# A four-layer transformer block in one kernel: first attention and first ffn with VectorE's side work moved and the up products computed a second time

## The reference, cut to what matters

```
# cond: x @ W_base + b_base + low rank part, weighted per batch
# attn: 16 heads of 8 features
q, k, v = proj(Wq) * mod, proj(Wk) * mod, proj(Wv) * mod
scores = einsum('bhid,bhjd->bhij', q, k) / sqrt(8) * cos_mat
w = softmax(scores); w = (w + roll(w, 1)) / sqrt(2)
x = x + einsum('bhij,bhjd->bhid', w, v) @ Wo

# cond2: a weight matrix per batch
w_bot = einsum('bg,got->bot', y, weight * mask)
y = einsum('bnt,bot->bno', x, w_bot) + bias

# ffn: everything is quantised with one scale per whole tensor
y = act_qdq(y)                      # scale = max(abs(y)) / 32767, round, scale back
up = act_qdq(y @ lpbq_dequant(w_up).T)      # 4 bit weights, a scale per 32 columns
gate = act_qdq(y @ lpbq_dequant(w_gate).T)
sig = fixed_qdq_u16(sigmoid(gate))
gate = act_qdq(gate * sig)
o = act_qdq(gate * up)
x = x + o @ lpbq_dequant(w_down).T
```

## Time and profile before

| what | value |
|---|---|
| median of 3 runs | 1338.44 us |
| lowest and highest run | 1337.14 and 1338.82 us |
| the profiled execution's own time | 1340.86 us |
| its span in the profile | 1339.0 us |
| PE, DVE, ACT, POOL busy in the span | 1201.0, 831.2, 652.2, 271.0 us |
| mean granted clock of PE | 0.98 of full |
| chain that ended last | PE 70%, DVE 18%, ACT 6% |
| first attention | about 24 to 157.4 us of the span |
| from its end to the first gate product | 157.4 to 166.3 us |
| first ffn | 166.3 to about 244 us |

### The profile page before, as it was taken

How to read it: one execution, slowest core, us unless ns; L and a number is a source line. 1 busy time by engine, 2 the same in 40 slices (tenths; PEclk the granted TensorE clock), 3 DMA queues, 4 the chain that set the end, 5 groups by cost and what they waited for, 6 DMA issues and landing times.

```text
span 1339.0 us, 28276 instructions
## 1 busy us (share of the span) xinstructions
PE 1201.0 (90%) x10379; PEld 965.6 (72%) x10379; DVE 831.2 (62%) x1749; ACT 652.2 (49%) x1334; POOL 271.0 (20%) x349
## 2 busy tenths in 40 slices
PE   5898762889999899999999999889999999989999
PEld 3666520458878789887887888479889866657777
DVE  4988678564555566657777565466564477764342
ACT  2766587345434234443454444234434467746553
POOL 4666200210004142330000014043330021200000
PEclk9999985999999999999999999999999999999999
DMA  9000100501312123104106101032102000000000
GB/s 328 2 2 2 49 31 0 212 0 64 133 81 89 52 64 98 48 25 161 53 17 257 48 8 50 22 94 78 44 20 88 1 2 3 3 3 0 1 16 16
DMA packets 42901, 75.86 MB, mean 57 GB/s; under 512 B 3849, under 2 KB 33809, under 8 KB 41873
## 3 DMA queue, kind: packets, MB, share of 16 engines
q1 hardware_dynamic: 38672, 65.66, 13.5%
q0 software_dynamic: 4096, 8.40, 2.1%
HBM read 59.75 MB, written 14.29 MB: 55 GB/s over the span
## 4 chain that ended last, share of the span: by engine, by line
PE 70%; DVE 18%; ACT 6%; issue 3%; DVEq 1%; DMA 1%; POOL 0%; ACTq 0%; SPq 0%; POOLq 0%
PE banks L1949 7%; PE banks L1960 7%; PE banks L1945 7%; PE banks L2004 5%; PE banks L1936 4%; PE banks L2014 3%; PE banks L1690 3%; PE banks L1685 3%; PE banks L1692 3%; PE banks L1691 3%; PE banks L1929 2%; PE banks L1931 2%; PE banks L1930 2%; DVE SM L2395 2%; PE banks L1816 2%
## 5 line engine op out<-in xcount | busy, mean ns | idle before, releaser
L2203 ACT ACTIVATE SC<-banks 128x512 f32<-128x512 f32 x192 | 114.4, 596 | 225.2 <-PE banks L1945 126.3
L2290 DVE SCALAR_TENSOR_TENSOR SC<-banks,SM,SC 128x512 f32<-128x512 f32 x128 | 95.9, 749 | 121.3 <-PE banks L1949 102.8
L1960 PE MATMUL banks<-A,SC 128*128 x1024 | 137.0, 277 | 8.3 <-DVE SC L2290 7.6
L1949 PE MATMUL banks<-X,SC 128*128 128x128 f32 x1024 | 136.9, 277 | 4.5 <-DVE SC L2569 3.2
L1945 PEld LDWEIGHTS banks<-X,SC 128*128 128x128 f32 x1024 | 126.1, 192 | 19.5 <-issue 12.5
L1945 PE MATMUL banks<-X,SC 128*128 128x128 f32 x1024 | 136.1, 276 | 4.4 <-ACT SC L2187 3.2
L1960 PEld LDWEIGHTS banks<-A,SC 128*128 128x128 f32 x1024 | 125.4, 192 | 17.8 <-issue 16.9
L1949 PEld LDWEIGHTS banks<-X,SC 128*128 128x128 f32 x1024 | 124.5, 192 | 6.9 <-DVE SC L2569 5.9
L2004 PE MATMUL banks<-A 128*128 128x128 f32 x736 | 100.0, 279 | 13.7 <-DVE A L2719 8.1
L2004 PEld LDWEIGHTS banks<-A 128*128 128x128 f32 x736 | 89.3, 191 | 19.1 <-ACT A L2228 9.7
L2187 ACT ACTIVATE SC<-A 128x512 f32 x128 | 80.6, 630 | 28.4 <-PE banks L1949 23.3
(11 more groups left out here) (342 smaller groups left out, 2518.0 us busy)
## 6 DMA issues: line engine op xcount, KB each, us to landing
A<-in_moe SPq DMA_DIRECT2D x36, 768.0 KB, 10.6
A<-xs SPq DMA_DIRECT2D x20, 256.0 KB, 3.9
ys<-A SPq DMA_DIRECT2D x20, 256.0 KB, 2.3
BW<-in_l1f SPq DMA_DIRECT2D x2, 2048.0 KB, 7.9
BW<-in_l2f SPq DMA_DIRECT2D x1, 3456.0 KB, 11.1
BW<-in_l1c SPq DMA_DIRECT2D x1, 3072.0 KB, 17.3
BW<-in_l3f SPq DMA_DIRECT2D x1, 2816.0 KB, 10.1
A<-in_l1c SPq DMA_DIRECT2D x1, 2560.0 KB, 8.7
```

Of the source, the lines that this page charges most:

```text
L1949: m = e.matmul(at["pu"].ap[:, cut(q)], wx[:, cut(4 + q)], x, start=True, stop=True)
L1960: m = e.matmul(o, at["h"].ap[:, cut(q)], W[:, bass.ds(r + (1024 + 128 * q), 128)], start=k == 0 and q == 0, stop=k == 1 and q == 3)
L2203: e.activation(at["h"].ap, at["pg"].ap, ACT.Gelu_apprx_tanh).then_inc(at["gelu"][0], 1)
L2290: return e.scalar_tensor_tensor(out=o, in0=a, scalar=s, in1=b, op0=o1, op1=o2)
```

## The change

1. `fq`: of the seven weight quantisation steps only the first three stay on DVE; the divide and the last multiply go to POOL, the two roundings to ACT (with a bias tile ROUND that POOL fills at the start).
2. `route_steps`: the maxima and the first eight index pairs are issued before the first conditioning product of chunk 0 is finished; the other eight and the difference behind half step 1, the mixing behind half step 2. Before they were behind half steps 23 to 27.
3. `cond2` for chunks 0, 1 and 2 is issued inside the attention, in the second half of head groups 5, 9 and 13, in a bank of RB0, and waits for its own part of WBOT; their three maxima at head group 16. Only chunk 3 stays behind the attention.
4. In the first halves of head groups 5, 9 and 13 the output product of the finished chunk is issued ahead of the value products of the group before.
5. Up products are not copied to SBUF: DVE takes the maximum from the bank, the bank is freed, and `upq` computes the same product a second time, with ACT quantising from the bank into UU.

The diff, cut to its core:

```
@@ first_half, second_half
                 if p < 16:
                     parts[p, 0][0]()
+                if p >= 5 and p % 4 == 1:
+                    parts["out", p // 4 - 1]()
                 if p:
                     parts[p - 1, 0][2]()
                     parts[p - 1, 1][2]()
-                if p >= 5 and p % 4 == 1:
-                    parts["out", p // 4 - 1]()
...
+                if p == 16:
+                    for n in range(3):
+                        y_max(n)
                 if p:
                     parts[p - 1][1]()
                 for f in todo.get(2 * p + 1, []):
                     f()
+                if p >= 5 and p % 4 == 1:
+                    cond2(p // 4 - 1, RB0)
@@ before the attention
+        rt = route_steps()
+        rt[0]()
+        rt[1]()
         last()
...
-                        at = step("fq", k=k, raw=raw, mx=mx, iv=iv, prev=u["t"])
-                        at["t"] = u["t"] = tick("fq")
+                        at = step("fq", k=k, raw=raw, mx=mx, iv=iv, prev=u["t"], on=("vec", "vec", "vec", "pool", "act", "act", "pool")[k])
+                        at["t"] = u["t"] = tick("fq_" + at["on"])
...
+        beside_heads[1] += rt[2:4]
+        beside_heads[2] += rt[4:5]
-        for k, f in enumerate(fs + rt):
+        for k, f in enumerate(fs):
             beside_heads[3 + k].append(f)
+        def cond2(n, ring):
+            at = step("cond2", n=n, x=sig["x0", n], wbot=sig["wb", 4 * n], pa=ring.take(), yfree=sig["Yfree", n])
...
+        items.append(([("x0", 3)], [lambda: cond2(3, RA)], ("y0b", 3)))
@@ up products
             at["mm"] = sig["Yfree", n] = tick("f0_mm")
-            at["ev"] = tick("f0_act")
-            RA.give(at["pa"], at["ev"])
+            if m < 3:
+                at["ev"] = tick("f0_act")
             at["t"] = tick("f0_vec")
+            RA.give(at["pa"], at["ev"] if m < 3 else at["t"])
...
-            at = step("upq", Uq=Uq, ui=up_scale["inv"], ready=up_scale["t"])
+            at = step("upq", n=n, m=m + 3, Uq=Uq, ui=up_scale["inv"], ready=up_scale["t"], pa=RA.take())
+            at["mm"] = sig["Yfree", n] = tick("f0_mm")
             at["t"] = tu[n, m] = tick("f0_act")
+            RA.give(at["pa"], at["t"])
@@ ScalarE, VectorE, GpSimd
+                    e.activation(at["raw"], at["raw"], ACT.Identity, bias=ROUND[:, at["k"] - 4:at["k"] - 3]).then_inc(at["t"][0], 1)
...
-                    e.activation(at["Uq"], at["Uq"], ACT.Identity, scale=at["ui"], bias=MAG).then_inc(at["t"][0], 1)
+                    w.wait_ge(*at["mm"])
+                    e.activation(at["Uq"], v4(at["pa"].ap), ACT.Identity, scale=at["ui"], bias=MAG).then_inc(at["t"][0], 1)
...
+                        w.wait_ge(*at["mm"])
+                        absmax(at["mx"], v4(at["pa"].ap)).then_inc(at["t"][0], 1)
...
+                    e.tensor_tensor(r3, r3, bc_last(at["iv"] if at["k"] == 3 else at["mx"], 32), ALU.mult).then_inc(at["t"][0], 1)
```

More of the change, by code:

```diff
@@ L640, in build @@
         at["m"], t_mod = tick("prep_dve"), tick("mod")
-        last()
-        done.add(("y0", 0))
-        attn = mh_attn(0, "y0", "x0", cond0)
         t_idx, t_ww = (S_("idx"), 1), (S_("ww"), 1)
@@ L726, in build @@
         items += attn
-        for n in range(NC):
-            def c2(n=n):
-                at = step("cond2", n=n, x=sig["x0", n], wbot=sig["wbot"], pa=RA.take(),
-                          yfree=sig["Yfree", n])
-                at["mm"] = sig["wbot_over"] = tick("c2_mm")
-                at["y"] = sig["y0b", n] = tick("c2_y")
-                RA.give(at["pa"], at["y"])
-            items.append(([("x0", n)], [c2], ("y0b", n)))
+        items.append(([("x0", 3)], [lambda: cond2(3, RA)], ("y0b", 3)))
         in_order(items, done)
@@ L772, in build @@
         t_mag = tick("f0_vec")
-        for n in range(NC):
-            at = step("f0_ymax", n=n, y=sig["y0b", n], mx=mx[:, n:n + 1])
-            at["t"] = tick("f0_vec")
-        scl, inv, t = scale_of(mx, 4, at["t"])
+        y_max(3)
+        scl, inv, t = scale_of(mx, 4, sig["ymax"])
         tq = []
```

48 lines of the change are left out of this document (32 added, 16 removed).

## The result

| | kernel before | changed kernel |
|---|---|---|
| median | 1337.79 us (4 runs, 1336.8 to 1338.82) | 1320.46 us (4 runs, 1317.24 to 1323.03) |
| ratio of the times | 1 | 0.9872, 95% interval 0.9854 to 0.989 |
| the profiled execution's own time | 1340.86 us | 1317.24 us |
| its span | 1339.0 us | 1315.4 us |

The change makes the kernel 1.3% faster, 17.3 us by the medians, where 15.5 us were forecast (1323 us). The profiled executions differ by more, 23.6 us. So the first thing to do is to cut both spans at the same events: the starts of the first, second and third score products, the end of the last normalisation (L2408, now L2431), the first gate product (L1845, now L1860) and the first residual add of the ffn (L2488, now L2507). All times are us.

A forecast was written before the change was run, and what follows sets the result against it. The prediction saw TensorE and VectorE both near full in the attention loop; attention 8.9, between stages 1.8 and ffn 4.8 sum to 15.5 us, from the 1338.44 us median to 1323 us, range 1315 to 1331.

The forecast's parts named there:

- Rivals 1: Attention: TensorE bounds it, only 2 us of its waits come back; 10.2 us gained, 1328 us; chance 0.22.
- 2 (22.9 us): Attention: VectorE is the sole bound, so all work it sheds counts; 22.9 us gained, 1315.5 us; chance 0.15.
- The start of the attention: First score chunks: moved routing delays VectorE's maximum and exp; a loss of 1.9 us (0.7 to 2.8).
- 1.2 us pass straight through: Ahead of the second scores: index and difference on VectorE delay the score products by their full 1.2 us.
- rival 4: TensorE's clock stays low: its idle stretches move, both drops show elsewhere; 12.4 us gained, 1326 us; chance 0.06.
- The middle: Attention, 32 to 130 us: TensorE's waits give back 5.6 us (2 to 6.0), the clock 1.7 us (0 to 1.7).
- The hole at the fifteenth scores: Attention from 130 us: scores start 4.8 us earlier, plus 1.4 us of clock; gain 6.2 us (4.8 to 6.2).
- Conditioning products: Three moved into the attention: 2.7 us lost there (0 if in holes), 1.8 us gained between the stages (1 to 2).
- The ffn: Up maxima no longer wait for ScalarE's copies, second products hidden; gain 4.8 us (3.5 to 5.5).
- rival 5: Attention: GpSimd's added instructions make scaled keys late, holding score products; 20.8 us lost, 1344 us; chance 0.04.
- Rival 3: The lock: GpSimd's 5.3 us of multiplications hit VectorE's SBUF work one for one; 10.2 us gained, 1328 us; chance 0.05.
- a part of the same 5.6 us: Attention, 32 to 130 us: the earlier output product's 2.0 us was counted within the 5.6 us of returned TensorE waits.

The follow-up runs named there:

- e11: Changed kernel plus three matmuls with unread results ahead of the second scores, in a bank nobody had used; ratio 0.9856 to the kernel before.
- e2: Changed kernel with the output product behind the value products again in head groups 5, 9 and 13; ratio 0.9925 to the kernel before.
- e8: Changed kernel with the router's maxima, indices and mixing back behind half steps 23 to 27; ratio 0.9895 to the kernel before.
- e3: Changed kernel with the three conditioning products and their maxima behind the attention again; ratio 0.9866 to the kernel before.
- e5: Changed kernel with up products copied to SBUF by ScalarE again and computed only once; ratio 0.9903 to the kernel before.
- e1: Changed kernel with all seven weight quantisation steps on VectorE again; ratio 0.9903 to the kernel before.
- e4: Changed kernel with maxima, index pairs, difference and its exp ahead of the last piece before the attention, mixing in the first half step; ratio 0.9886 to before.
- e9: The changed kernel itself, run again on another chip; 1321.47 us against 1336.4 us before, ratio 0.9882.
- e6: Changed kernel plus seven matmuls with unread results ahead of the second scores, in a bank of RB; ratio 0.9908 to the kernel before.
- e12: Kernel before with only the output products moved ahead of the value products in head groups 5, 9 and 13; ratio 0.9969 to the kernel before.
- e7: As e4, but the difference and its exp stand behind the last piece before the attention; ratio 0.9837 to the kernel before.
- e10: Changed kernel with the edits of e7 and e3 together; 1315.66 us, ratio 0.9843 to the kernel before.

## Why the prediction was right, and where not

**The sum.** 15.5 us were forecast, the edited stretches gave 14.1, the times 17.3 on one chip and 14.9 on another. The likeliest case was the one that happened: VectorE's chain paced the attention, TensorE's waits could be had back, and the ffn's maxima waited for ScalarE. Rivals 1 (10.2 us) and 2 (22.9 us) lie further from the 14.1 us. That the sum came so near is in part luck: 2.35 us too little were put down as lost at the start, 0.85 too little as won in the middle and 0.4 too little in the ffn, and these partly cancel. The times' 17.3 us have in them what the unedited parts did.

**The start of the attention** is the term that failed: a loss of 1.9 us (0.7 to 2.8) was forecast, 4.25 us came. Without the clock the sum was right and its terms were not: 1.75 us came where "1.2 us pass straight through" stood (0.55 of it is the difference's longer duration), and 0.2 us for the mixing where 0.7 stood (e11's third scores, at full clock, 7.36 us behind the second against 7.15 before). What I had not counted is what the longer wait does: TensorE stood 4.17 instead of 2.42 us, fell to half clock behind it, and e11 measured that as 2.3 us. I had taken back two such drops as gains, and had not asked whether the change makes one. "Clock 1.00 through the attention" was wrong for that reason, and rival 4 (both drops show elsewhere) was half right: one did.

**The middle**, third to fourteenth scores: 5.6 us of waits and 1.7 of clock less 1.8 for two conditioning products made 5.5 us; 89.92 us became 83.57, 6.35 less. The waits of the earlier trace rows are gone as listed above. The clock of 105 to 109 us is 1.00.

**The hole at the fifteenth scores**: 4.8 us forecast from the two value products and the mixing, 4.85 measured (11.32 us between the fourteenth and fifteenth scores became 6.47). The parts bear it out: the output product back made it 8.55 us (e2, 2.1 more), the routing back 8.96 (e8, 2.5 more). Behind it the forecast had 1.4 us of clock less one conditioning product, and 17.94 us became 17.48.

**Conditioning products**: a loss of 2.7 us in the attention, a gain of 1.8 between the stages. e3 measured 2.0 and 1.5, the latter where the clock stays. The sign of the sum, against this part of the change, was right.

**The ffn**: 4.8 us forecast (3.5 to 5.5), 5.2 measured, and e5 gives all of it to the one edit. The second products were hidden. Whether they would be without the store of banks wasn't tried.

**What GpSimd and ScalarE took over** was hidden as forecast: four multiplications of 0.83 to 1.49 us and four roundings of 0.60 to 1.02 us, and no engine waited for one of the multiplications. GpSimd did stand 7.8 us for VectorE before the first of them (45.51 us), twice what rival 5 had priced, but no score product waited for keys behind it, so rival 5 did not happen. Rival 3 (the lock, one for one) falls by e1.

**Who deserves the credit** I had wrong inside a right sum. I wrote the middle's gain to the quantisation, maxima and indices that leave VectorE, and called the output product "a part of the same 5.6 us". By the runs of one part each: the output product's place 4.9 us, the routing 6.9 us less 4.25 at the start, the quantisation 2.6 us, the conditioning products -2.0 and +1.5, and the ffn's edit 5.2. The largest net part in the attention, 4.9 us, is an edit that takes no work from any engine: it only lets VectorE have its operand earlier. 7.8 us of work taken off an engine that is 90% busy from 32 to 130 us gave 2.6 us, a third of the work's own length.

**A rule and its row.** The Trainium skill, Perfetto Trace Analysis, section Optimizing Scalar/DVE Operations, gives VectorE some 65 ns more of access overhead on PSUM than on SBUF; the forecast had set 0.8 us of loss by it beside the sum. In the changed kernel the same reduction of 512 columns takes 684 ns from banks and 680 from SBUF (the two groups L2316 above): 0.05 us over 12. Here the measurement decides, and the ffn gained 5.2 us, not 4.0.

## What to carry to other kernels

Before moving work off a busy engine, look where that engine waits: three output products issued 2 us earlier each were worth about twice as much (4.9 us) as 7.8 us of work removed (2.6 us). When work is moved into the wait of another engine, ask how long TensorE stands still afterwards, since a wait that grows from 2.4 to 4.2 us costs its length and then once more in clock. And follow each piece of a moved step on every queue: an exp of 16 columns on ScalarE cost 2 us because a copy that all depended on stood behind it (e4).

## What the runs showed of the hardware

**The clock behind a wait.** Ahead of the second scores TensorE stood idle 4.16 to 4.18 us in six profiles (changed, e1, e2, e3, e5, e9), and the clock fell in all of them, as it did behind 4.96 us in e6. With 1.59 us (e11) and 2.4 us (before, e8, e12) it stayed. With 2.62 to 2.64 us it stayed once (e7) and fell twice (e4, e10). Elsewhere it also fell behind shorter waits: behind 1.91 us ahead of the eleventh scores of the kernel before, and around the last output product, where TensorE stands 1.41 and 0.88 us, in three profiles of ten (e2, e5, e9). So the length of the last wait alone doesn't decide, and what else does stays open. How long it then stays low varies too: the second stretch took from 8.56 to 9.89 us with the same instructions. So a kernel whose waits are of this size has a spread that its code does not explain, and a gain of 1.5 us can come or go. The combination of e7 with e11's filler wasn't run.

**Small instructions that take 1 us.** The mixing was costed at 2.8 us from the earlier trace rows. It is about 1 us of work, and the rest is VectorE standing in its own instruction. In the changed kernel L2373 on 16 columns runs from 30.72 to 31.70 us and L2313 on 32 columns from 31.95 to 33.09; the same step took 0.19 us in the kernel before (L2290), and there it was L2350 and L2352 that took 1 us each. GpSimd's timeline of the changed kernel has the ends:

```profile
30.62 1.04 POOL L2905 TENSOR_TENSOR A<-A,CC 128x512 f32<-128x512 f32 x1
31.75 1.29 POOL L2909 TENSOR_TENSOR A<-A 128x512 f32<-128x512 f32 x1
```

They end at 31.66 and 33.04 us, within 0.05 us of VectorE's two. The Trainium skill, SBUF — State Buffer, section Who interferes with whom, says that a VectorE instruction with two SBUF inputs contends with a GpSimd instruction that reads SBUF; by that rule, the trace agrees. (L2352, in the kernel before, has only one SBUF input and took 0.98 us too, so two inputs aren't the only case here.) The difference L2365 of the start is a third such row: it ended at 28.45 us, 0.05 us behind a GpSimd instruction, and it cost 0.55 us on the chain. So rival 3's mechanism is there, but the rows that show it are short ones: they took up to 1 us more than at their quickest. Which of them pays changes with when it falls (L2365 took 0.73 us in the changed kernel and 0.17 in e4). It is argued from these coinciding ends, not shown: nothing that was run here took GpSimd's work away to price it.

**Stages that nobody edited** took 1093.7 to 1103.2 us in the profiles. On the chip of e9 to e12 it was 1094.2 to 1096.6, on that of e1 to e8 1097.9 to 1103.2. What makes the difference stays open; the difference of two spans alone, 23.6 us here, would have credited the change with 7.7 us that are not its own.
